# Graph channels and gate logits of a 16-group ViT tower kernel in fp16 passes, with a second ReLU for the high parts and a moved transpose step

## The chip, the cores and the metric

The kernel runs on one core of a Trainium2 chip. The metric is device time in microseconds, the median of several executions. PE is TensorE (PEld its weight loads), ACT ScalarE, DVE VectorE, POOL GpSimd, SP SyncE. TensorE's clock has two levels here, 2.4 and 1.2 GHz, which the profile shows as a granted clock of 1.00 and 0.50.

## The reference, cut to what matters

64 images of 2x104x104 become 169 tokens each of width 128, and a class token makes 170. Then two residual blocks follow:

```python
h = h + _L0_attn_ref(_layernorm(h, axis=-1), ...)
h = h + _L0_ffn_ref(_layernorm(h, axis=-1), ...)
```

The first is a graph convolution with 4 channels over the 128 features and a projection:

```python
h = jax.nn.relu(_gcn_conv(x, W1, b1, src, dst, norm))      # 4 channels
h = _gcn_conv(h, W2, b2, src, dst, norm)
x_combined = jnp.concatenate([x_enc[..., None], gcn_output], axis=-1)
x_projected = x_combined @ Wp.T + bp
```

The second is causal attention (2 heads of 64, normalised queries and keys) followed by a mixture of 8 experts of width 512, all of them computed and weighed by a softmax gate:

```python
gate = jax.nn.softmax(y @ gate_W + gate_b, axis=-1)
hid = jax.nn.gelu(jnp.einsum('bnd,edf->bnef', y, W1) + b1)
eo = jnp.einsum('bnef,efd->bned', hid, W2) + b2
out = jnp.einsum('bned,bne->bnd', eo, gate)
```

## The kernel before, in words

Features lie on the 128 partitions, tokens on the free axis. The 64 images are cut into 16 groups of 4 (T = 680 tokens, two halves of 340). A prologue of some 160 us builds all tokens (patch convolution) and folds the weights of the graph block into matrices: `adj` for the graph product, `plain` for the direct part and `gcn_m`, four 128x128 fp32 matrices, one for each channel. Then for each group g there is `attention(g)` and `ffn(g)`, written out for each engine as its own program; the order on an engine is the order of these calls, and semaphores tie them together. Groups 2 and on run in loops.

Most products are split by hand: an fp32 matrix becomes a high and a low fp16 part, and three fp16 passes (high by high, high by low, low by high) replace one fp32 product. Before the change the graph channels and the gate logits are still fp32.

The FFN is made of 32 slots, one for each 128-wide chunk of an expert's hidden layer, and 3 more (`LAG`). In slot s PE runs `experts_in(s)` (six products into one of two PSUM pairs, line 979), ACT runs a GELU into fp32 (line 620) and, in three slots of four, a second GELU into the fp16 high part (line 625, `hi`), DVE makes the low part (line 1395) and in the fourth also the high one, and PE runs `experts_out(s - 3)` (line 998). After each 4 chunks DVE weighs an expert's output (`weigh`, line 1408) and GpSimd adds it to the output by a DMA (line 459). In slots 32 and 33 PE runs the attention scores of the next group (`scores`, line 889), whose two PSUM pairs are free once the high GELUs of slots 30 and 31 are done.

Work for later groups hangs on the slots, by tables: `LN2_SLOTS` and `QK_SLOTS` (second layer norm, queries and keys of group g+1) and `EARLY_SLOTS` (fixing the tokens, first layer norm, graph product and ReLUs of group g+2). All of it shares one PSUM pair, `fr_ps`. An entry is run behind the slot's own work on each engine that has a part in it. `edges` (slot 28) leaves the graph product in `fr_ps`, and `relu0` to `relu3` read it on ACT (line 548), each with its own scale and bias, into `h1`.

`attention(g)` on PE is a list: `plain` and channel step 0 of group g+1 (line 759, all by way of `both`), `values` (line 871), step 1, the transposes of the probabilities of images 0 and 1 (`turn_probs`, line 904), step 2, `weigh(0)` (line 916), transposes, `weigh(1)`, transposes, step 3, `weigh(2)`, `project(0)` (line 923), `weigh(3)`, `mean2`, `project(1)` and then the logits (line 961), eight fp32 products of 85 tokens by 8 gates. On ACT it is 16 exponentials (line 584; they need DVE's maxima, and a table load goes ahead of the first), then a load of the GELU table, the evacuations of the attention output and of y, a square, and the tanh of the gates. On DVE it is `normalise(0)`, `normalise(1)`, the copies of the values, `normalise(2)`, the copies of the transposed probabilities, and so on; then `h2`, `y_parts` (y in fp16 parts, lines 1323 and 1325) and the softmax of the gates (lines 1354 to 1373). The transposes of image 0 wait for its normalised probabilities and for the first copy of the values. The first transposes of the layer norm roots (`cast_roots`, line 787) wait for DVE's inverse roots.

```python
                graph_of("plain", 0)
                for b in range(NB):
                    values(g, b, later)
                graph_of(1)
                turn_probs(g, 0)
                turn_probs(g, 1)
                graph_of(2)
                weigh(g, 0)
```

## Time and profile before

| what | value |
| --- | --- |
| median of 3 executions | 1547.23 us (1546.29 to 1547.50) |
| profiled execution, whole | 1546.54 us |
| its span | 1544.4 us |
| PE busy | 1480.5 us, 96% of the span |
| DVE busy | 1214.5 us, 79% |
| ACT busy | 1083.9 us, 70% |
| POOL busy | 192.8 us, 12% |
| chain of waits, share of PE | 67% |
| mean granted clock | 0.984 |

An engine's busy time is the union of its instructions. A row of the timeline gives the start of a run of instructions, its length, the engine and line, what is written from what, how many, and in brackets the idle time ahead of it with what ended it. PE rows overlap a little, since a matmul's end is modelled: the distance from one start to the next is the better price.

### The profile page before, as it was taken

The numbers are of one execution on the slowest core, as the hardware profiler recorded it, in microseconds if no ns is written. First come the engines' busy times: TensorE is split into PE (matmuls) and PEld (weight loads), VectorE is DVE, ScalarE is ACT, GpSimd is POOL, SyncE is SP. The second block draws the span as 40 slices with busy tenths as digits, with TensorE's granted clock in tenths as the row PEclk, the third lists the DMA queues.
The fourth block names the chain that finished last, engine by engine and source line by source line (L and its number), as shares of the span: only waits on it lengthen the run. The fifth ranks groups of instructions, "written<-read, shape, count | busy, mean of one in ns | idle before, by whom it ended". The sixth has DMA issues, their size and how long they took to land.

```text
span 1544.4 us, 31017 instructions
## 1 busy us (share of the span) xinstructions
PE 1480.5 (96%) x10879; PEld 1016.1 (66%) x10879; DVE 1214.5 (79%) x2567; ACT 1083.9 (70%) x1861; POOL 192.8 (12%) x223
## 2 busy tenths in 40 slices
PE   6898899999999999999999999999999999999998
PEld 4554666666666666666666666666666667667665
DVE  6768798878788787878788787888788787877765
ACT  5232577777777777786777777786777777777756
POOL 1134042010101010110101010110101010100101
PEclk9999899999999999999999999999999999999989
DMA  7866053333323242433233242433333242434334
GB/s 242 200 149 145 1 164 46 100 45 100 45 77 68 28 116 37 104 44 102 40 95 50 37 107 36 109 45 100 45 97 46 56 85 34 110 44 104 52 92 55
DMA packets 40339, 125.54 MB, mean 81 GB/s; under 512 B 5744, under 2 KB 5744, under 8 KB 38128
## 3 DMA queue, kind: packets, MB, share of 16 engines
q0 software_dynamic: 22464, 55.81, 26.0%
q1 hardware_dynamic: 17696, 69.28, 12.5%
q8 instruction: 19, 0.31, 0.1%
q14 instruction: 16, 0.13, 0.0%
q10 hardware_dynamic: 144, 0.01, 0.0%
HBM read 68.98 MB, written 50.48 MB: 77 GB/s over the span
## 4 chain that ended last, share of the span: by engine, by line
PE 67%; DVE 22%; issue 6%; ACT 4%; DVEq 1%; DMA 1%; POOLq 0%; ACTq 0%
PE pair L998 21%; PE pair L979 17%; PE pair L759 10%; DVE area L1395 6%; PE pair L746 4%; PE pair L916 3%; PE pair L904 2%; DVE root_t L1230 2%; PE pair L889 2%; DVE area L1408 2%; DVE area L1393 2%; PE pair L923 2%; PE pair L840 1%; PE pair L787 1%; PE pair L871 1%
## 5 line engine op out<-in xcount | busy, mean ns | idle before, releaser
L620 ACT ACTIVATE area<-pair,pack_b_sb 128x680 f32<-128x680 f32 x512 | 422.4, 828 | 219.6 <-PE pair L979 215.0
L1395 DVE TENSOR_TENSOR area<-area 128x680 f16<-128x680 f32 x512 | 445.5, 873 | 142.9 <-ACT area L625 138.2
L998 PE MATMUL pair<-area,ws 128*128 128x340 f16 x3072 | 527.2, 307 | 13.0 <-DVE area L1408 12.0
L979 PE MATMUL pair<-area,ws 128*128 128x340 f16 x3072 | 526.3, 308 | 0.4 <-ACT area L625 0.4
L998 PEld LDWEIGHTS pair<-area,ws 128*128 128x128 f16 x3072 | 286.8, 98 | 171.3 <-DVE area L1408 44.7
L979 PEld LDWEIGHTS pair<-area,ws 128*128 128x128 f16 x3072 | 297.3, 98 | 143.6 <-ACT area L625 0.5
L625 ACT ACTIVATE area<-pair,pack_b_sb 128x680 f16<-128x680 f32 x384 | 316.0, 823 | 0.0
L459 POOL DMA_DIRECT2D tower_out<-area x128 | 109.5, 855 | 1215.0 <-DVE area L1408 1162.9
L1408 DVE SCALAR_TENSOR_TENSOR area<-pair,pack_b_sb,area 128x340 f32<-128x340 f32 x256 | 134.0, 565 | 15.6 <-PE pair L998 15.3
L584 ACT ACTIVATE area<-pair,nbias,root 85x85 f32<-85x85 f32 (+1 forms) x256 | 112.3, 466 | 3.0 <-DVE nbias L1298 3.0
L746 PE MATMUL pair<-area,pack_a_sb 128*128 128x392 f32 (+1 forms) x260 | 96.0, 514 | 17.5 <-DVE area L1217 14.4
L746 PEld LDWEIGHTS pair<-area,pack_a_sb 128*128 128x128 f32 x260 | 50.9, 206 | 54.6 <-DVE area L1217 26.6
L759 PE MATMUL pair<-area,gcn_m 128*128 128x340 f32 x256 | 86.6, 462 | 0.0
L1393 DVE CAST area<-area 128x680 f16<-128x680 f32 x128 | 66.8, 522 | 20.6 <-ACT area L620 14.5
L548 ACT ACTIVATE area<-pair,pack_b_sb 128x680 f32<-128x680 f32 x64 | 59.1, 933 | 15.9 <-PE pair L759 15.3
L1217 DVE TENSOR_TENSOR area<-area,pack_a_sb 128x728 f32<-128x728 f32 x65 | 61.7, 996 | 0.3 <-PE pair L746 0.3
L598 ACT ACTIVATE area<-pair 128x340 f32<-128x340 f32 x32 | 14.5, 453 | 64.0 <-PE pair L923 64.0
L1310 DVE TENSOR_SCALAR area<-area,rs 85x85 f32<-85x85 f32 (+1 forms) x256 | 55.7, 278 | 2.3
L584 ACT ACTIVATION_READ_ACCUMULATOR area<-pair,nbias,root 85x1 f32 x256 | 55.2, 215 | 0.0
L528 ACT ACTIVATE ht<-pair 128x392 f32<-128x392 f32 (+1 forms) x26 | 19.8, 871 | 50.2 <-PE pair L746 50.2
L1317 DVE COPY area<-pair 85x510 f32<-85x510 f32 x64 | 42.4, 681 | 16.0 <-PE pair L904 16.0
L759 PEld LDWEIGHTS pair<-area,gcn_m 128*128 128x128 f32 x256 | 44.9, 192 | 13.9 <-issue 0.5
(209 smaller groups left out, 1634.4 us busy)
## 6 DMA issues: line engine op xcount, KB each, us to landing
tower_out<-area POOLq DMA_DIRECT2D x128, 340.0 KB, 4.6
area<-gate_scratch SPq DMA_DIRECT2D x16, 1360.0 KB, 10.0
area<-gate_scratch SPq DMA_DIRECT2D x16, 1020.0 KB, 7.2
area<-cells SPq DMA_DIRECT2D x16, 392.0 KB, 5.3
area<-cells POOLq DMA_DIRECT2D x14, 392.0 KB, 6.6
area<-area POOLq DMA_DIRECT2D x14, 392.0 KB, 4.8
tower_out<-ht SPq DMA_DIRECT2D x16, 340.0 KB, 2.3
area<-gate_scratch SPq DMA_DIRECT2D x16, 340.0 KB, 4.6
```

The costliest lines, as they stand in the source:

```text
L459: pool.dma_start(out[:, g * T:(g + 1) * T], tmp[e % 2], accum_op=ALU.add).then_inc(out_done, 16)
L584: nc.scalar.activation(probs[:, b * SCORE + o0:b * SCORE + o0 + w], score_ps_at(b)[:, h, c * QC:c * QC + w], ACT.Exp, bias=nbias[:, n:n + ...
L620: nc.scalar.activation(two(hid[slot % NHID]), halves(hid_ps[slot % 2]), ACT.Gelu_apprx_tanh, bias=col(COL_B1 + slot)).then_inc(hid_ready, 1)
L625: nc.scalar.activation(two(hh[slot % NPART]), halves(hid_ps[slot % 2]), ACT.Gelu_apprx_tanh, bias=col(COL_B1 + slot)).then_inc(hhi_act, 1)
L746: last = mm(cells_ps(p, j), conv_w[:, shift * D:(shift + 1) * D], xg[n % XG][:, c0 * BZ:c1 * BZ], start=(shift == 0), stop=(shift == SHIFT ...
L759: last = mm(fr_ps[:, j, 0:TH], lhs, rhs[:, j, :], start=start, stop=stop)
L979: last = mm(hid_ps[slot % 2][:, j, 0:TH], lhs[:, w], rhs[:, j * TH:(j + 1) * TH], start=(i == 0), stop=(i == 2))
L998: last = mm(eo_ps[:, j, 0:TH], lhs[:, w], rhs[:, j * TH:(j + 1) * TH], start=(m % CH == 0 and i == 0), stop=(m % CH == CH - 1 and i == 2))
L1217: v.tensor_tensor(xg[n % XG].rearrange("p (j b) -> p j b", b=BZ), src[:, c0 * BZ:(c0 + NP) * BZ].rearrange("p (j b) -> p j b", b=BZ), gv, ...
L1393: v.tensor_copy(hh[slot % NPART], hid[slot % NHID]).then_inc(hhi_dve, 1)
L1395: v.tensor_tensor(hl[slot % NPART], hid[slot % NHID], hh[slot % NPART], ALU.subtract).then_inc(hlo_ready, 1)
L1408: v.scalar_tensor_tensor(tmp[e % 2][:, j * TH:(j + 1) * TH], eo_ps[:, j, 0:TH], b2_s[:, e:e + 1], gbc[:, e * T + j * TH:e * T + (j + 1) * ...
```

## The change

- The four channel steps of groups 2 to 15 run in three fp16 passes: `gcn_h` and `gcn_l` by `h1_h` and `h1_l`. Groups 0 and 1 keep the fp32 path (`later` is false).
- For these groups ACT computes every ReLU twice, into fp32 buffers that are free then (`relu`) and into the fp16 high part `h1_h`. GpSimd subtracts the two into `h1_l` (`relu_parts`), channel 0 behind the output DMA of expert 5, channels 1 to 3 behind that of expert 6.
- The ReLUs move from slots 28, 29, 30, 31 to 29, 31, 32, 33; ACT's `ffn` now has 35 slots, the last three with no GELU.
- `fix0` and `fix1` move from slots 5 and 6 to 6 and 7.
- The logits leave `attention` for slot 0 of the FFN, by halves of four tiles, each ahead of that half's expert products: y_high by [W_high | W_low] (16 columns) and y_low by W_high (8 columns). They wait for `yl` and not for `y32`. DVE adds the two column groups with one more reduction.
- PE's `cast` of the second layer norm goes behind `experts_out` in its slot.
- `gcn_h`, `gcn_l` and `gate_hl` are made in the prologue, by GpSimd (two operations) and DVE (two).

```diff
--- before.py
+++ after.py
@@ -60,9 +60,9 @@
 GATE_SLOTS = {"turn": 2, "turned": 0}
 QK_SLOTS = {"q": 7, "sums_q": 9, "k": 9, "sums_k": 11, "root0": 11, "root1": 11, "root2": 12, "wide": 14,
             "cast": 16, "kn": 15}
-EARLY_SLOTS = {"fix0": 5, "fix1": 6, "fix2": 8, "fix3": 9, "tok_hi": 11, "mean": 18, "dev": 17, "sq": 19,
+EARLY_SLOTS = {"fix0": 6, "fix1": 7, "fix2": 8, "fix3": 9, "tok_hi": 11, "mean": 18, "dev": 17, "sq": 19,
                "var": 21, "root0": 21, "root1": 21, "root2": 22, "cast": 25, "xn": 24, "xn_lo": 25, "edges": 28,
-               "relu0": 28, "relu1": 29, "relu2": 30, "relu3": 31}
+               "relu0": 29, "relu1": 31, "relu2": 32, "relu3": 33}
 SUMS_AT = T // 2
 
 FIRST_0 = {"tail": 4, "fix0": 5, "fix1": 5, "fix2": 6, "fix3": 6, "mean": 7, "dev": 9, "sq": 10, "var": 11, "root0": 13,
...
@@ -209,8 +211,10 @@
 
         at[0] = 0
         dev, sq, h1 = take(T), take(T), take(4 * T)
+        h1_h, h1_l = (h1[:, 2 * n * T:2 * (n + 1) * T].bitcast(F16) for n in range(2))
         sqk, fix = h1[:, 0:T], h1[:, T:T + NB * NP * NP]
         xh, qs, kb, sqq = (take(T) for _ in range(4))
+        relu = (xh, sqq, dev, sq)
         xh_h, xh_l = take(T // 2).bitcast(F16), take(T // 2).bitcast(F16)
         part_h, part_l = take(T // 2).bitcast(F16), take(T // 2).bitcast(F16)
         k_wide = take(TILES * 128)[0:QC, :]
...
@@ -417,6 +422,11 @@
             def tokens_lo(g):
                 pool.wait_ge(tokh_ready, g - 1)
                 pool.tensor_tensor(two(part_l), tokens(g), two(part_h), ALU.subtract).then_inc(tokl_ready, 1)
+
+            def relu_parts(g, c):
+                half = slice(c * T, (c + 1) * T)
+                pool.wait_ge(h1_ready, 4 * g + c + 1)
+                pool.tensor_tensor(h1_l[:, half], relu[c], h1_h[:, half], ALU.subtract).then_inc(relu_lo, 1)
 
             def split(e):
                 pool.wait_ge(w_in[e], 32)
...
@@ -447,6 +457,10 @@
                     split(W_SPLIT.index(a))
             for e in range(len(W_SPLIT), 4):
                 split(e)
+            pool.wait_ge(dve_prep, PREP_DVE)
+            pool.tensor_copy(gcn_h[:, :], gcn_m[:, :]).then_inc(gcn_split, 1)
+            pool.wait_ge(gcn_split, 1)
+            pool.tensor_tensor(gcn_l[:, :], gcn_m[:, :], gcn_h[:, :], ALU.subtract).then_inc(gcn_split, 1)
 
             def weigh(g, later=True, ahead=True):
 
...
@@ -461,6 +475,9 @@
                         split(e + 4)
                     if e == 1 and ahead:
                         tokens_lo(g + 2)
+                    if e in (E - 3, E - 2) and ahead:
+                        for c in ((0,), (1, 2, 3))[e - E + 3]:
+                            relu_parts(g + 2, c)
 
             for g in range(G):
                 weigh(g, later=g > 0, ahead=g < G - 2)
...
@@ -533,7 +550,7 @@
                 nc.scalar.activation(root_in[:, ROOTS[kind]], fr_ps[0:QC, 0, first:first + n], ACT.Identity,
                                      bias=eps[0:QC, at:at + 1], scale=scale).then_inc(var_out[kind], 1)
 
-            def early(g, step):
+            def early(g, step, later=True):
                 if step == "tok_hi":
                     act.wait_ge(fixed, NB * (g + 1))
                     nc.scalar.activation(two(part_h), tokens(g), ACT.Copy).then_inc(tokh_ready, 1)
...
@@ -545,8 +562,11 @@
                 if step[:4] == "relu":
                     c = int(step[4])
                     act.wait_ge(g_ps, g + 1)
-                    nc.scalar.activation(two(h1[:, c * T:(c + 1) * T]), halves(fr_ps), ACT.Relu,
-                                         bias=scal[:, 4 + c:5 + c], scale=scal[:, c:c + 1]).then_inc(h1_ready, 1)
+                    dst = relu[c] if later else h1[:, c * T:(c + 1) * T]
+                    for part in (dst, h1_h[:, c * T:(c + 1) * T])[0:2 if later else 1]:
+                        last = nc.scalar.activation(two(part), halves(fr_ps), ACT.Relu,
+                                                    bias=scal[:, 4 + c:5 + c], scale=scal[:, c:c + 1])
+                    last.then_inc(h1_ready, 1)
 
             def graph(g, step):
                 if step == "sq2":
...
@@ -609,7 +629,7 @@
                 y_evac(g, 1)
                 if ahead:
                     graph(g + 1, "sq2")
-                act.wait_ge(lg_step, 3 * (g + 1))
+                act.wait_ge(lg_step, 4 * (g + 1))
                 nc.scalar.activation(lge[:, :], lg[:, :], ACT.Tanh, scale=0.5).then_inc(lge_ready, 1)
 
             def experts(g, slot):
...
@@ -626,8 +646,9 @@
                                          bias=col(COL_B1 + slot)).then_inc(hhi_act, 1)
 
             def ffn(g, ahead):
-                for slot in range(SLOTS):
-                    experts(g, slot)
+                for slot in range(SLOTS + LAG):
+                    if slot < SLOTS:
+                        experts(g, slot)
                     for step in steps_in(LN2_SLOTS, slot):
                         graph(g + 1, step)
                     for step in steps_in(QK_SLOTS, slot):
...
@@ -638,13 +659,13 @@
 
             def chain(n):
                 for step in steps_in(FIRST_0, n):
-                    early(0, step)
+                    early(0, step, later=False)
                 for step in steps_in(GRAPH_0, n):
                     graph(0, step)
                 for step in steps_in(QK_0, n):
                     queries_keys(0, step)
                 for step in steps_in(FIRST_1, n):
-                    early(1, step)
+                    early(1, step, later=False)
 
             sums_first()
             act.wait_ge(pack_b_in, 16)
...
@@ -808,16 +829,23 @@
                     pe.wait_ge(xnl_ready, g + 1)
                     of_xn(adj_h[:, :], adj_l[:, :]).then_inc(g_ps, 1)
 
-            def graph(g, step):
+            def graph(g, step, later=True):
                 if step == "plain":
                     pe.wait_ge(split_step, 4)
                     pe.wait_ge(h1_ready, 4 * (g + 1))
                     of_xn(plain_h[:, :], plain_l[:, :], stop=False)
-                if step in range(4):
+                if step in range(4) and later:
+                    w, src = slice(step * D, (step + 1) * D), slice(step * T, (step + 1) * T)
+                    pe.wait_ge(gcn_split, 2)
+                    pe.wait_ge(relu_lo, 4 * (g - 2) + step + 1)
+                    both(gcn_h[:, w], two(h1_h[:, src]), start=False, stop=False)
+                    both(gcn_h[:, w], two(h1_l[:, src]), start=False, stop=False)
+                    last = both(gcn_l[:, w], two(h1_h[:, src]), start=False, stop=(step == 3))
+                if step in range(4) and not later:
                     last = both(gcn_m[:, step * D:(step + 1) * D], two(h1[:, step * T:(step + 1) * T]),
                                 start=False, stop=(step == 3))
-                    if step == 3:
-                        last.then_inc(gcn_ps, 1)
+                if step == 3:
+                    last.then_inc(gcn_ps, 1)
                 if step == "mean2":
                     pe.wait_ge(h2_ready, g + 1)
                     both(mean_m[:, :], tokens(g)).then_inc(mean2_ps, 1)
...
@@ -931,7 +959,7 @@
                 def graph_of(*steps):
                     if ahead:
                         for step in steps:
-                            graph(g + 1, step)
+                            graph(g + 1, step, later)
 
                 if not later:
                     for m in range(NB // 2):
...
@@ -954,12 +982,15 @@
                 graph_of("mean2")
                 project(g, 1)
 
-                pe.wait_ge(pt_ready, NB * (g + 1))
-                for t in range(TILES):
-                    if t % NB == 0:
-                        pe.wait_ge(y_ready, 2 * g + t // NB + 1)
-                    last = mm(eo_ps[0:QC, 0, t * E:(t + 1) * E], y32[:, t * QC:(t + 1) * QC], gate_ws,
-                              start=True, stop=True)
+            def logits(g, j):
+
+                if j == 0:
+                    pe.wait_ge(pt_ready, NB * (g + 1))
+                pe.wait_ge(yl_ready, 2 * g + j + 1)
+                for t in range(j * NB, (j + 1) * NB):
+                    c, y = 2 * t * E, slice(t * QC, (t + 1) * QC)
+                    mm(eo_ps[0:QC, 0, c:c + 2 * E], yh[:, y], gate_hl[:, :], start=True, stop=False)
+                    last = mm(eo_ps[0:QC, 0, c:c + E], yl[:, y], gate_hl[:, 0:E], start=False, stop=True)
                 last.then_inc(logit_ps, 1)
 
             def experts_in(g, slot):
...
@@ -974,7 +1005,7 @@
                 w = slice(slot * D, (slot + 1) * D)
                 for j in range(2):
                     if slot == 0:
-                        pe.wait_ge(yl_ready, 2 * g + j + 1)
+                        logits(g, j)
                     for i, (lhs, rhs) in enumerate(((w1h, yh), (w1h, yl), (w1l, yh))):
                         last = mm(hid_ps[slot % 2][:, j, 0:TH], lhs[:, w], rhs[:, j * TH:(j + 1) * TH],
                                   start=(i == 0), stop=(i == 2))
...
@@ -1006,7 +1037,8 @@
                     if slot < SLOTS:
                         experts_in(g, slot)
                         for step in steps_in(LN2_SLOTS, slot):
-                            graph(g + 1, step)
+                            if step != "cast":
+                                graph(g + 1, step)
                         for step in steps_in(GATE_SLOTS, slot):
                             gates(g, step)
                         for step in steps_in(QK_SLOTS, slot):
...
@@ -1018,12 +1050,14 @@
                         scores(g + 1, slot - SLOTS, True)
                     if slot >= LAG:
                         experts_out(g, slot - LAG)
+                    if slot == LN2_SLOTS["cast"]:
+                        graph(g + 1, "cast")
 
             def chain(n):
                 for step in steps_in(FIRST_0, n):
                     early(0, step, later=False)
                 for step in steps_in(GRAPH_0, n):
-                    graph(0, step)
+                    graph(0, step, later=False)
                 for step in steps_in(QK_0, n):
                     queries_keys(0, step)
                 for step in steps_in(FIRST_1, n):
...
@@ -1103,6 +1137,10 @@
                     v.tensor_copy(hi[:, :], src).then_inc(split_step, 1)
                     dve.wait_ge(split_step, 2 * p - 11)
                     v.tensor_tensor(lo[:, :], src, hi[:, :], ALU.subtract).then_inc(split_step, 1)
+                if p == 9:
+                    v.tensor_copy(gate_hl[:, 0:E], gate_ws).then_inc(split_step, 1)
+                    dve.wait_ge(split_step, 9)
+                    v.tensor_tensor(gate_hl[:, E:2 * E], gate_ws, gate_hl[:, 0:E], ALU.subtract).then_inc(split_step, 1)
                 if p == 7:
                     v.tensor_scalar(gq[:, 0:1], col(COL_QN), float(DH) ** 0.5, None, ALU.mult).then_inc(dve_prep, 1)
                     dve.wait_ge(dve_prep, 21)
...
@@ -1349,13 +1387,15 @@
                     graph(g + 1, "dev2")
                 y_parts(g, 1)
 
-                dve.wait_ge(logit_ps, g + 1)
+                dve.wait_ge(logit_ps, 2 * (g + 1))
                 lg3 = lg[:, :].rearrange("p (t e) -> p t e", e=E)
-                v.tensor_tensor(lg3, eo_ps[0:QC, 0, 0:TILES * E].rearrange("p (t e) -> p t e", e=E),
-                                gate_bs.unsqueeze(1).broadcast_to([QC, TILES, E]), ALU.add).then_inc(lg_step, 1)
-                dve.wait_ge(lg_step, 3 * g + 1)
+                v.tensor_reduce(lg3, eo_ps[0:QC, 0, 0:2 * TILES * E].rearrange("p (t n e) -> p t e n", n=2, e=E),
+                                AX.X, ALU.add).then_inc(lg_step, 1)
+                dve.wait_ge(lg_step, 4 * g + 1)
+                v.tensor_tensor(lg3, lg3, gate_bs.unsqueeze(1).broadcast_to([QC, TILES, E]), ALU.add).then_inc(lg_step, 1)
+                dve.wait_ge(lg_step, 4 * g + 2)
                 v.tensor_reduce(gm[:, 0:TILES], lg3, AX.X, ALU.max).then_inc(lg_step, 1)
-                dve.wait_ge(lg_step, 3 * g + 2)
+                dve.wait_ge(lg_step, 4 * g + 3)
                 v.tensor_tensor(lg3, lg3, gm[:, 0:TILES].unsqueeze(2).broadcast_to([QC, TILES, E]),
                                 ALU.subtract).then_inc(lg_step, 1)
                 dve.wait_ge(lge_ready, g + 1)
```

## Rows read from the trace of the kernel before

**Rows 1.** A steady group's stretch: us, busy of PE, PEld, DVE, ACT, POOL, clock, DMA.

```profile
773.00:859.00 86.00, 84.71 (x660) 58.80 (x658) 69.36 (x150) 64.91 (x112) 8.30 (x9) 1.00 0.35 69
```

**Rows 2.** Timeline of the first attention, ACT and PE: start us, us, engine, line.

```profile
168.41 0.42 ACT L584 ACTIVATE area<-pair,nbias,root 85x85 f32<-85x85 f32 x1
...
173.88 1.99 PE L904 MATMUL pair<-ident,area 85*85 85x85 f32 x12 [4.48 <-DVE area L1329]
175.66 2.54 PE L759 MATMUL pair<-area,gcn_m 128*128 128x340 f32 x4
...
185.72 1.48 PE L961 MATMUL pair<-pack_b_sb,area 128*85 128x8 f32 x16
```

**Rows 3.** Timeline of the last attention, ACT and PE.

```profile
1459.30 0.42 ACT L584 ACTIVATE area<-pair,nbias,root 85x85 f32<-85x85 f32 x1
...
1464.76 1.60 PE L904 MATMUL pair<-ident,area 85*85 85x85 f32 x12 [2.43 <-DVE area L1329]
...
1476.66 2.37 PE L961 MATMUL pair<-pack_b_sb,area 128*85 128x8 f32 x16
```

**Rows 4.** Timeline of ACT at the end of a steady FFN.

```profile
768.72 0.92 ACT L548 ACTIVATE area<-pair,pack_b_sb 128x680 f32<-128x680 f32 x1
769.52 0.83 ACT L620 ACTIVATE area<-pair,pack_b_sb 128x680 f32<-128x680 f32 x1
770.23 0.84 ACT L625 ACTIVATE area<-pair,pack_b_sb 128x680 f16<-128x680 f32 x1
...
773.16 0.97 ACT L548 ACTIVATE area<-pair,pack_b_sb 128x680 f32<-128x680 f32 x1
774.14 1.28 ACT L584 ACT_TABLE_LOAD   x1
775.64 0.42 ACT L584 ACTIVATE area<-pair,nbias,root 85x85 f32<-85x85 f32 x1 [0.21 <-DVE nbias L1298]
```

**Rows 5.** Timeline of PE over the attention that follows it.

```profile
771.51 1.12 PE L889 MATMUL pair<-area 64*85 64x85 f32 x16
...
776.95 0.74 PE L759 MATMUL pair<-area,plain_h 128*128 128x340 f16 x4
777.82 1.30 PE L759 MATMUL pair<-area,gcn_m 128*128 128x340 f32 x4
778.97 0.28 PE L871 MATMUL pair<-wv_h,area 128*85 128x128 f16 x2
...
781.50 1.07 PE L904 MATMUL pair<-ident,area 85*85 85x85 f32 x12
...
786.00 1.34 PE L759 MATMUL pair<-area,gcn_m 128*128 128x340 f32 x4
787.28 0.66 PE L916 MATMUL pair<-area 85*64 85x170 f32 x8
...
791.04 1.48 PE L961 MATMUL pair<-pack_b_sb,area 128*85 128x8 f32 x16
...
794.11 1.30 PE L771 MATMUL pair<-mean_m,area 128*85 128x1 f32 x16
```

**Rows 6.** Same timeline, DVE; then two groups by line: busy, mean ns, idle before.

```profile
792.10 0.51 DVE L1325 TENSOR_TENSOR area<-area 128x340 f16<-128x340 f32 x1
...
L787 PE MATMUL pair<-ident,root 85*128 85x85 f32 x256 | 24.8, 240 | 8.0 <-DVE root L1234 8.0
...
L419 POOL TENSOR_TENSOR area<-ht,area 128x680 f16<-128x680 f32 x14 | 20.6, 1470 | 18.7 <-ACT area L539 18.7
```

**Rows 7.** PE idle in the prologue, and stretches of 1 us with the clock.

```profile
66.69 6.96 PE L746 MATMUL pair<-area,pack_a_sb 128*128 128x392 f32 x12 [1.73 <-ACT ht L528]
...
66.00:67.00 1.00, 0.31 (x1) 0.34 (x2) 1.00 (x3) 1.00 (x3) 0.00 (x0) 0.52 0.90 276
...
178.00:179.00 1.00, 1.00 (x10) 0.71 (x9) 0.00 (x0) 0.00 (x0) 0.00 (x0) 0.67 0.00 0
...
1482.00:1483.00 1.00, 1.00 (x7) 0.59 (x6) 0.97 (x2) 0.52 (x1) 0.00 (x0) 0.72 0.00 0
```

More of the change, by code:

```diff
@@ L140, in vit_tower @@
         gate_ws, gate_bs, b2_s = packs["gate_w"], packs["gate_b"][0:QC, :], packs["b2"]
+        gate_hl = sb("gate_hl", [128, 2 * E], F16)
         area = sb("area", [128, AREA])
@@ L157, in vit_tower @@
         gcn_m = sb("gcn_m", [128, 4 * D])
+        gcn_h, gcn_l = (sb(n, [128, 4 * D], F16) for n in ("gcn_h", "gcn_l"))
         gcn_c = sb("gcn_c", [128, 1])
@@ L264, in vit_tower @@
         g_ps, h1_ready, gcn_ps, h2_ready = map(sem, ("g_ps", "h1_ready", "gcn_ps", "h2_ready"))
+        relu_lo, gcn_split = map(sem, ("relu_lo", "gcn_split"))
         mean2_ps, dev2_ready, sq2_ready, var2_ps = map(sem, ("mean2_ps", "dev2_ready", "sq2_ready", "var2_ps"))
```

## The prediction

> **What bounds the kernel now.** I read the table of stretches first: in one steady group PE is busy 84.71 of 86.00 us at a granted clock of 1.00 (2.4 GHz), DVE 69.36, ACT 64.91 [rows 1]. The exponentials of the first and of the last group start 1290.9 us apart [rows 2, 3], 86.06 us for each of 15 groups, and nearly all of that is PE. Then I read the end of one FFN and the attention after it in the timeline, on ACT [rows 4] and on PE [rows 5]. The reader should see that the exponentials are already on the edge. In the steady group they start at 775.64 and PE begins the transposes of the first probabilities at 781.50, 5.86 us later [rows 4, 5]. In the first and last attention, where PE stands waiting for them (idle 4.48 and 2.43 us), the distance is 5.47 and 5.46 us [rows 2, 3]: four exponentials, four more, two normalisations, one copy of the values, all in order. So the steady group has 0.4 us of slack there, and a later exponential soon becomes PE's wait.
>
> **Graph channels.** A channel step was two fp32 products of two records each, four records: 777.82 to 778.97, 1.15 us [rows 5]. Three fp16 passes are six records like the three passes ahead of it (776.95 to 777.82, 0.87 us). Saved are 0.29 us a step, and 0.41 us where the fp32 step held up the weights behind it (step 3: 786.00 to 787.28 is 1.28 us). The new path is taken in 14 attentions (g = 1 to 14): at least 14 x 4 x 0.29 = 16 us, if PE stays the bound.
>
> **The ReLUs on ACT.** Four become eight. One takes 0.80 us from start to start (768.72 to 769.52 [rows 4]). The f16 copy may be nearer a GELU's 0.71 us; I take 0.80, since the nearest row is the same ReLU. Before, relu1 and relu2 sit between hi(29) and GELU(31), and relu3 follows hi(31). After, relu0's two lie before GELU(30), and GELU(31) starts where it did. But hi(30), which scores(0) waits for, moves from 770.23 to 771.03 and ends at 771.87, while scores(0) started at 771.51 [rows 5]: PE waits 0.4 us. After hi(31) there were one ReLU, the table load and the first exponential. Now there are six: first at 773.16, last at 777.16, table load at 778.14, exponential at 779.42. The exponentials start **3.8 us later**; before, nothing but the maxima (0.21 us of idle) held them [rows 4].
>
> **What PE does meanwhile.** It reaches `plain` at 777.4 (776.95 and the 0.4), waits for the last ReLU until 778.2, and runs plain 0.87, step 0 0.87, values 1.33 (the 2.53 us between 778.97 and 781.50 [rows 5], less a step of 1.20, between the two seen), step 1 0.87: done at 782.15. It can transpose at 779.42 + 5.47 = 784.9, so it idles 2.7 us, and that stage starts **3.4 us late**. Steps 0 and 1 save time only inside this wait. Step 2 is swallowed too, since `weigh` behind it waits for the probabilities. Step 3 gives back 0.4. The logits' place comes 3.0 us late.
>
> **GpSimd.** Four subtractions like the one at 1.47 us [rows 6]. relu_parts(0) has its input near 770.3, before attention begins; parts 1 to 3 end near 779.6 (778.14 + 1.47), and the step that needs part 1 comes at 781.3, the others after the wait. Queued behind them on GpSimd is only expert 7's output DMA, up to 1.5 us late; what it frees is written again for expert 1 of the next FFN, slots later. Without that cover a group would pay up to the 1.5. The two preparations of gcn_h and gcn_l and DVE's two small ones lie in a prologue where GpSimd idles: nothing. The bound on the other side is the next row: 4 x 1.47 on the path, 5.9 us a group, for which I see no way.
>
> **Logits.** Before: 16 fp32 records from 791.04, then slots 0 and 1 of the FFN, until 794.11: 3.07 us [rows 5], of which 12 products take 12 x 0.145 = 1.73 and the records 1.34. After: eight fp16 records for a half, 0.45 us (0.056 each: `values` has 24 such weights in 1.33; the fp32 record's 0.084 is the upper bound), three products 0.43, then the second half, which waits for yl. That comes with DVE's subtraction, 792.10 + 0.51 = 792.61 [rows 6], 1.6 us after the start. So 1.62 + 0.45 + 0.43 + 0.87 = 3.37 us: 0.3 **lost**, not gained. The DVE chain to the gates could start at 792.61 and now starts 0.7 us later (791.04 + 2.07 + the matmul's end, 0.2), with one small reduction more, a shape no row has: I put it at 0.25, half of that 0.51 us subtraction, from nothing to the whole, so gates, GELU(0) and out(0) come about 1.0 us later. Queued behind the new wait for yl are only the second half of slot 0 and what follows it.
>
> **Cast.** The eight transposes waited 8.0 us in 15 groups [rows 6], 0.53 each. Behind experts_out(1) that wait is gone, and covers about what the later gates cost: at slot 5 PE is 0.25 behind before. The extra products ahead of the transposes delay hx by less than DVE's own lag. fix0 and fix1 change places on DVE, which has 16.6 us free a group [rows 1]: nothing, and if DVE were late at weigh(0), at most the lag of 1.0 us.
>
> **Sum without the clock:** 3.41 - 0.41 + 0.25 = 3.25 us a group, x 14 = 45.5.
>
> **The clock.** An idle stretch of 1.73 us in the prologue left the clock at half (mean 0.52 in that microsecond), so did the 4.48 and the 2.43 [rows 2, 3, 7]. I expect 2.7 us, with 0.8 just before, to do it in most groups. In the first attention the clock came back during 178 to 179 (0.67), 4.5 us after PE resumed. There PE took 11.84 us from transposes to logits, against 9.54 in the steady group [rows 2, 5]: 2.30 more. A step at half clock was 2.47 there and will be 1.73 in fp16, so 1.56 us a group, x 14 = 21.8.
>
> **Total:** 45.5 + 21.8 = 67.3. The profiled execution took 1546.54 (span 1544.4 and 2.1 around it): 1613.8. The median of three is 0.7 above it, so I say **1615 us**. From both sides: if f16 ReLUs take 0.71, 14 x 3 x 0.09 = 4 us less; if no group loses the clock, 22 less.
>
> **A rule weighed.** The table load takes 1.28 us, 774.14 to 775.42, and the first exponential starts at 775.64 as soon as the maxima are there; at the end it starts at 1459.30, 0.02 after the load. The Trainium skill, "ScalarE: Activation LUTs", section "What ACT_TABLE_LOAD costs", adds a drain of about 1380 ns to each switch. By it the exponentials would start 1.38 us later still, 19 us in all, 1634. The rows show no such time after the load; I go by the rows.
>
> **Rivals.**
> - *The clock stays low.* In the last attention PE also resumed after 2.43 us, and the clock came back only in 1482 to 1483 (0.72), 17 us later [rows 7]; transposes to logits took 11.90 us with no graph work in it. For it: fp16 steps give PE shorter stretches of dense work than the fp32 step that stood before the return in the first attention. Against it: the last one has idle gaps that graph work fills. From transposes to logits 9.54 - 0.8 = 8.7 us of work would double; if the clock returns with the dense products just before the logits, some 6.9 of it: 14 x (3.25 + 6.9) = 142 us, 1689. Chance 0.22, and part of it would show as a time between 1615 and 1689.
> - *No fall.* 1592 us. For it: 2.7 us lies between busy stretches at full clock. Chance 0.18.
> - *Faster: the exponentials do not decide.* Place: PE's wait for the first transposes. It decides as soon as ACT's extra work is above the 0.4 us of slack. If it stayed below (ReLUs overlapped with PE's other work, the table load off the path), PE would keep its 16 us and the 8 of the cast: 1523. Against it: in-order ACT with six ReLUs ahead. Chance 0.07, with 0.01 of it within 0.2%.
> - *Change without effect*: it would need the ReLUs to stand behind the exponentials; the ACT program has slots 32 and 33 ahead of attention. Under 0.01.
>
> The forecast itself has 0.53.
>
> **Range.** From 1586, below the case without a fall by 3 us for cheaper ReLUs and 3 for logits, to 1685, just inside the worst of the low clock. About 3 us, 0.2%, is what a measurement can tell from no change. Faster 0.06, within 0.01, slower 0.93.
>
> **What would show it.** Right: exponentials starting 3.8 us after where they stood relative to hi(31), six ReLU rows before the table load; a PE wait near 2.7 us at L904's counterpart, in 14 groups; windows of half clock in the attentions; logits in two parts with a wait for yl; no wait at the ln2 transposes; group period near 91 us. Wrong: a steady PE busy share of 98% as before, or fp16 steps standing unbroken in front of transposes that wait for nothing.

## The result, and the profile after

The changed kernel takes **1622.85 us** (median of 4, 1615.83 to 1630.71) against 1547.03 for the one before. The ratio, estimated from the single executions, is 1.0497, 95% interval 1.0473 to 1.0521. The forecast was 1615 in a range of 1586 to 1685.

The profile page of the changed kernel, its span and parts 1 and 2 (the clock in tenths):

```profile
span 1621.4 us, 31400 instructions
PE 1498.3 (92%) x10991; PEld 1011.4 (62%) x10991; DVE 1233.3 (76%) x2585; ACT 1125.5 (69%) x1917; POOL 276.3 (17%) x281
...
PEclk9998999999989999999999899999999899999989
```

PE's busy time is 18 us longer (1498.3 for 1480.5), though it has less to do: in a version below with the same products, whose clock held, it is 1461.4. Its share of the longer span has fallen from 96% to 92%. So the 77 us by which the span grew (1621.4 for 1544.4) are time in which PE waits or runs at half clock.

The end of an FFN and the attention after it in the changed kernel, ACT and PE, the counterpart of [rows 4] and [rows 5]. The last line is PE at the second half of the logits:

```profile
342.56 1.12 PE L917 MATMUL pair<-area 64*85 64x85 f32 x16 [0.35 <-ACT area L645]
343.07 0.87 ACT L645 ACTIVATE area<-pair,pack_b_sb 128x680 f16<-128x680 f32 x1
343.79 5.01 ACT L567 ACTIVATE area<-pair,pack_b_sb 128x680 f32<-128x680 f32 x6
...
348.81 1.28 ACT L604 ACT_TABLE_LOAD   x1
348.85 0.75 PE L780 MATMUL pair<-area,plain_h 128*128 128x340 f16 x4 [0.68 <-ACT area L567]
349.44 0.45 PE L780 MATMUL pair<-area,plain_l 128*128 128x340 f16 x2
349.73 0.74 PE L780 MATMUL pair<-area,gcn_h 128*128 128x340 f16 x4
350.11 0.42 ACT L604 ACTIVATE area<-pair,nbias,root 85x85 f32<-85x85 f32 x1
...
355.57 1.19 PE L932 MATMUL pair<-ident,area 85*85 85x85 f32 x12 [2.60 <-DVE area L1367]
...
366.33 0.21 PE L992 MATMUL pair<-gate_hl,area 128*85 128x16 f16 x1 [0.71 <-DVE area L1363]
```

The last high GELU of the FFN in the kernel before:

```profile
772.45 0.86 ACT L625 ACTIVATE area<-pair,pack_b_sb 128x680 f16<-128x680 f32 x1
```

In the changed kernel six ReLUs stand in a row behind the last high GELU (343.07), then the table load, then the first exponential (350.11), 7.04 us after that GELU's start. Before, it was 3.19 us (772.45 to 775.64 [rows 4]). PE waits four times: 0.35 us at the first scores, 0.68 at `plain`, 2.60 at the first transposes, which start 5.46 us after the exponentials, and 0.71 at the second half of the logits.

All 14 changed attentions show these rows. They differ in what follows. From the transposes to the first logits took 9.14 us in five of them, 12.1 in six and 15.3 in three; before it was 9.54. Stretches of two attentions; the clock is in the third column from the right:

```profile
534.00:545.00 11.00, 8.37 (x89) 6.51 (x88) 7.51 (x27) 9.73 (x36) 1.66 (x2) 1.00 0.22 32
...
446.00:452.00 6.00, 6.00 (x37) 4.24 (x36) 3.59 (x10) 2.42 (x5) 0.00 (x0) 0.53 0.00 0
452.00:458.00 6.00, 6.00 (x25) 3.33 (x24) 1.89 (x4) 1.00 (x2) 0.00 (x0) 0.50 0.00 0
```

The first line is an attention without a fall (its transposes start at 540.07). The other two are one whose transposes start at 444.76, whose clock fell at 446.4 and came back only 13.7 us later. The distance from one attention's exponentials to the next is 89.12 us where the clock held, some 92.1 and 95.3 where it fell, 86.03 before.

The span's 77.0 us, by those distances: 13 x 3.09 = 40.2 without the clock; 36.4 from it (6 x 2.98 + 3 x 6.18); 7.2 in the interval of the first FFN; 0.2 and 1.0 less in the last two stretches; and 5.5 **less** in the prologue, up to the first exponential.

Of the 7.2 us in the first FFN, 3.8 are the ReLUs, 2.1 a longer wait for DVE's weigh of one expert (4.74 for 2.62), and behind that wait the clock was at 0.50 from 218 to 221, which it was not before. That leaves 1.3 us for it; a fall of this length cost 1.5 in a kernel below:

```profile
218.06 1.88 PE L1029 MATMUL pair<-area,ws 128*128 128x340 f16 x6 [4.74 <-DVE area L1448]
...
218.00:221.00 3.00, 2.94 (x11) 1.61 (x12) 2.96 (x3) 1.25 (x2) 2.14 (x3) 0.50 0.35 32
```

### The profile page after: what moved, and what is told of

Same layout as the page of the kernel before. It is cut to its first block, busy times and chain, and to the rows that moved or that the text cites. A ratio compares the mean times of both kernels' runs of the same rounds, so it can differ in the third digit from the quotient of the medians.

```text
span 1621.4 us, 31400 instructions
## 1 busy us (share of the span) xinstructions
PE 1498.3 (92%) x10991; PEld 1011.4 (62%) x10991; DVE 1233.3 (76%) x2585; ACT 1125.5 (69%) x1917; POOL 276.3 (17%) x281
## 4 chain that ended last, share of the span: by engine, by line
PE 59%; ACT 16%; DVE 16%; issue 7%; DMA 1%; DVEq 0%; ACTq 0%; POOLq 0%
PE pair L1010 18%; PE pair L1029 18%; PE pair L780 7%; ACT area L567 5%; ACT area L645 4%; ACT area L604 3%; PE pair L767 3%; DVE area L1435 3%; PE pair L944 3%; PE pair L932 3%; ACT area L640 2%; PE pair L808 2%; PE pair L951 2%; DVE root_t L1268 2%; DVE area L1448 2%
## 5 line engine op out<-in xcount | busy, mean ns | idle before, releaser
L640 ACT ACTIVATE area<-pair,pack_b_sb 128x680 f32<-128x680 f32 x512 | 422.4, 828 | 222.1 <-PE pair L1010 220.3
L1029 PE MATMUL pair<-area,ws 128*128 128x340 f16 x3072 | 528.0, 308 | 16.0 <-DVE area L1448 12.1
L567 ACT ACTIVATE area<-pair,pack_b_sb 128x680 f32<-128x680 f32 x120 | 101.0, 962 | 15.3 <-PE pair L780 15.3
L767 PE MATMUL pair<-area,pack_a_sb 128*128 128x392 f32 (+1 forms) x260 | 91.2, 493 | 17.8 <-DVE area L1255 14.7
L429 POOL TENSOR_TENSOR area<-area 128x680 f16<-128x680 f32 x56 | 82.3, 1470 | 122.4 <-ACT area L567 118.5
L932 PE MATMUL pair<-ident,area 85*85 85x85 f32 x384 | 51.2, 288 | 43.3 <-DVE area L1367 43.3
L932 PEld LDWEIGHTS pair<-ident,area 85*85 85x85 f32 x384 | 42.7, 190 | 53.5 <-DVE area L1348 48.5
L944 PEld LDWEIGHTS pair<-area 85*64 85x64 f32 x512 | 39.1, 172 | 29.7 <-issue 16.9
```

The source lines that it names most:

```text
L567: last = nc.scalar.activation(two(part), halves(fr_ps), ACT.Relu, bias=scal[:, 4 + c:5 + c], scale=scal[:, c:c + 1])
L640: nc.scalar.activation(two(hid[slot % NHID]), halves(hid_ps[slot % 2]), ACT.Gelu_apprx_tanh, bias=col(COL_B1 + slot)).then_inc(hid_ready, 1)
L767: last = mm(cells_ps(p, j), conv_w[:, shift * D:(shift + 1) * D], xg[n % XG][:, c0 * BZ:c1 * BZ], start=(shift == 0), stop=(shift == SHIFT ...
L932: last = tr(eo_ps[0:QC, b % 2, n * QC:(n + 1) * QC], probs[:, b * SCORE + n * QC:b * SCORE + (n + 1) * QC], ident[0:QC, 0:QC])
L1029: last = mm(eo_ps[:, j, 0:TH], lhs[:, w], rhs[:, j * TH:(j + 1) * TH], start=(m % CH == 0 and i == 0), stop=(m % CH == CH - 1 and i == 2))
```

## The experiments

Distances between exponentials ("group") are worked out from each kernel's timeline as above. They are less disturbed than the medians: the first exponential starts anywhere from 162.9 to 169.4 us in the twelve profiled kernels, and the wait in the first FFN lasts from 2.6 to 4.7 us, with no visible relation to the change that was made. Each kernel has one profiled execution, so waits, groups and falls of the clock are those of that one.

### A busy PE in place of the wait

```diff
                 graph_of(1)
+                if ahead and later:
+                    for _ in range(9):
+                        both(zero_h[:, :], two(h1_h[:, T:2 * T]), start=False, stop=False)
                 turn_probs(g, 0)
```

> The changed kernel, with 18 fp16 products of a zero matrix (2.6 us) put behind channel step 1 in 14 groups, into the sum that is open there, so that PE is busy where it waited 2.60 us and nothing else moves. If the low clock is what the five groups of 89.1 us lack and the nine of 92.1 and 95.3 have, all groups take 89.1 us and the time is 1623 - 36 = 1587 us, with low clock only in the first and last attention. If the low clock costs nothing because ACT and DVE set the pace there, the time stays at 1620 or above.

Measured: 1587.58 us (1585.8 to 1590.24), ratio 1.0272 (1.0242 to 1.0302). The added products and what follows, one attention:

```profile
441.45 2.77 PE L782 MATMUL pair<-area,zero_h 128*128 128x340 f16 x18
444.22 1.19 PE L934 MATMUL pair<-ident,area 85*85 85x85 f32 x12
...
438.00:456.00 18.00, 17.25 (x158) 12.25 (x157) 11.96 (x35) 11.99 (x40) 1.80 (x2) 1.00 0.14 19
```

The transposes still start 5.47 us after the exponentials, so nothing ahead of them moved. The clock stays at 1.00 in all 14, every transposes-to-logits distance is 9.14 and a group takes 89.1. So the low clock costs 35 us, it comes from PE's standing idle there, and the late exponentials themselves stay.

### Two ReLUs fewer on ACT

```diff
-                    for part in (dst, h1_h[:, c * T:(c + 1) * T])[0:2 if later else 1]:
+                    for part in (dst, h1_h[:, c * T:(c + 1) * T])[0:2 if later and c < 2 else 1]:
...
+                if c >= 2:
+                    pool.tensor_copy(h1_h[:, half], relu[c]).then_inc(relu_hi, 1)
+                    pool.wait_ge(relu_hi, 2 * (g - 2) + c - 1)
```

> The changed kernel, with the high parts of channels 2 and 3 made by a cast on GpSimd and not by a second ReLU on ACT: two ReLUs fewer between the last GELU and the exponentials. If the exponentials' start sets the attention, they come 1.6 us sooner, PE's idle before the transposes falls from 2.60 to 1.0 us, the clock stays at 1.00 and a group takes 89.1 - 1.6 = 87.5 us: 1547 + 14 x 1.5 and some 3 us in the first FFN, 1571 us. If the subtractions on GpSimd or the fp16 steps were the cost, the time stays above 1610.

Measured: 1582.27 us, the median of 1578.49, 1581.92, 1582.62 and one execution of 1856.62, which the ratio of 1.022 (1.0184 to 1.0256) leaves out. A group without a fall took 87.56 us: 1.56 less for two ReLUs, as the exponentials' start says. But the clock fell in 8 of 14:

```profile
354.66 1.19 PE L935 MATMUL pair<-ident,area 85*85 85x85 f32 x12 [1.69 <-DVE area L1370]
...
354.00:360.00 6.00, 5.34 (x40) 3.86 (x40) 4.68 (x15) 3.73 (x13) 0.00 (x0) 0.72 0.32 50
```

I had taken the 1.6 us off the idle time at the transposes alone. The 0.68 at `plain` went first, and 1.69 us stayed in one piece, after which the clock could still fall. Six falls cost 1.5 us each and two 3.0: 15 us together, which covers the miss of 11.

### The eight ReLUs back in slots 28 to 31

```diff
-               "relu0": 29, "relu1": 31, "relu2": 32, "relu3": 33}
+               "relu0": 28, "relu1": 29, "relu2": 30, "relu3": 31}
```

> The changed kernel, its eight ReLUs put back to slots 28 to 31. The second ReLUs of slots 29 and 30 now push the last GELU back by 1.6 us, but only two ReLUs stand behind it. If the exponentials' start is what counts, and not where the ReLUs stand, they come 1.6 us sooner than in the changed kernel, as with two ReLUs fewer: 87.5 us for a group without low clock. PE's idle is split (0.4 and 0.7 us at the scores, some 1.0 at the transposes), so the clock should fall in few groups: 1571 us, below the 1582 of the kernel with two ReLUs fewer. If the last GELU's lateness costs as much as the exponentials', 1590 us or more.

Measured: 1571.32 us (1567.74 to 1573.85), 1.0163 (1.0136 to 1.019). One attention:

```profile
694.90 1.12 PE L917 MATMUL pair<-area 64*85 64x85 f32 x16 [0.36 <-ACT area L645]
697.96 1.12 PE L917 MATMUL pair<-area 64*85 64x85 f32 x16 [0.65 <-ACT area L645]
706.59 1.19 PE L932 MATMUL pair<-ident,area 85*85 85x85 f32 x12 [1.02 <-DVE area L1367]
```

The same number of ReLUs as in the changed kernel, in the old slots, costs 51 us less than in the new ones. A group took 87.81, 1.31 less than the 89.12 of the changed kernel, and the clock fell in none of the 14. So the *place* of the ReLUs is the larger part of the loss only with the clock: it is worth 1.31 of the 3.09 us a group, and all of the 36 us of low clock.

The split of a wait seems to matter beside its sum. Here PE waits 2.23 us in four pieces (0.36, 0.65, 1.02, and 0.20 at `values`), with no fall in 14; with two ReLUs fewer it waited 2.04 us in two (0.35 and 1.69), with 8 falls in 14.

### No second ReLU: both parts on GpSimd

```diff
-                pool.tensor_tensor(h1_l[:, half], relu[c], h1_h[:, half], ALU.subtract).then_inc(relu_lo, 1)
+                pool.tensor_copy(h1_h[:, half], relu[c]).then_inc(relu_hi, 1)
+                pool.wait_ge(relu_hi, 4 * (g - 2) + c + 1)
+                pool.tensor_tensor(h1_l[:, half], relu[c], h1_h[:, half], ALU.subtract).then_inc(relu_lo, 1)
...
-                        for c in ((0,), (1, 2, 3))[e - E + 3]:
+                        for c in ((0, 1), (2, 3))[e - E + 3]:
```

ACT runs the four fp32 ReLUs alone, in slots 28 to 31.

> The changed kernel without any second ReLU: ReLUs back in slots 28 to 31, high and low parts both on GpSimd (a cast of about 1.2 us and the 1.47 us subtraction, four times, two behind expert 5's output and two behind expert 6's). The exponentials then start where they did before. PE cannot transpose sooner than 5.47 us after them (5.87 before), and the rest to the logits takes 9.14 for 9.54: 0.8 us a group gained, 0.1 lost with the logits: 85.3 us a group, 1547 - 10 = 1537 us, no low clock but in the first and last attention. Rival: GpSimd is too slow for the steps of the channels, PE waits for the fourth part and the time is 1550 or more.

Measured: 1542.37 us, 0.9983 (0.9969 to 0.9996), 85.80 us a group (85.3 expected; below, where the 0.5 went). Then the same with the old logits, in fp32 and in their old place:

> As the kernel with both parts on GpSimd, with the logits in fp32 in their old place. With the moved transposes the new logits cost only 0.1 us a group by the changed kernel's trace, so this is 1535 us. If they cost the 0.97 us a group that they cost alone, it is 1522 us.

Measured: **1530.94 us** (1526.87 to 1533.31), 0.9899 (0.9872 to 0.9925), 84.82 us a group. So the fp16 logits cost 0.98 us a group here, the second of the two expected cases. The median fell by 11 us and not by 15 or more; of the two profiled executions, this kernel's was 4.4 us longer in the prologue and the first FFN. This version is faster than both kernels. One attention of it:

```profile
683.22 0.96 ACT L567 ACTIVATE area<-pair,pack_b_sb 128x680 f32<-128x680 f32 x1
683.72 1.98 POOL L430 TENSOR_TENSOR area<-area 128x680 f16<-128x680 f32 x1
684.20 1.28 ACT L603 ACT_TABLE_LOAD   x1
685.65 0.74 POOL L428 CAST area<-area 128x680 f16<-128x680 f32 x1
686.47 1.47 POOL L430 TENSOR_TENSOR area<-area 128x680 f16<-128x680 f32 x1
687.01 0.95 DVE L1328 SCALAR_TENSOR_TENSOR nbias<-mx,root 85x8 f32<-85x8 f32 x1
687.88 1.04 DVE L1438 SCALAR_TENSOR_TENSOR area<-pair,pack_b_sb,area 128x340 f32<-128x340 f32 x2
688.85 0.16 DVE L1333 RECIPROCAL rs<-sm 85x4 f32<-85x4 f32 x1
...
691.65 1.19 PE L931 MATMUL pair<-ident,area 85*85 85x85 f32 x12 [0.52 <-DVE area L1359]
```

The same place in the kernel before:

```profile
776.86 0.16 DVE L1298 SCALAR_TENSOR_TENSOR nbias<-mx,root 85x8 f32<-85x8 f32 x1
776.96 1.05 DVE L1408 SCALAR_TENSOR_TENSOR area<-pair,pack_b_sb,area 128x340 f32<-128x340 f32 x2
777.93 0.16 DVE L1303 RECIPROCAL rs<-sm 85x4 f32<-85x4 f32 x1
```

GpSimd is in time for every step, and PE waits for none of its parts. But PE now waits 0.5 us at the transposes, which start 5.87 us after the exponentials and not the 5.47 expected. The last channel's subtraction on GpSimd lies beside DVE's work here. DVE's small product of the maxima (`nbias`) takes 0.95 us for 0.16 and ends at 687.96, 0.02 after the subtraction (686.47 + 1.47). The weigh of the last expert, the normalisations and the copy of the values, which the transposes wait for, stand behind it in DVE's order: the copy starts 5.03 us after the exponentials, against 4.64 before.

An attention has two such products. One of them is held in two other kernels as well, each time to the end of a subtraction on GpSimd within 0.02 us: the second for 1.02 us with two ReLUs fewer, the first for 0.75 with the ReLUs in the old slots, where the exponentials wait for it 0.3 us behind the table load (the 87.81 us a group for the 87.5 expected). The weigh is not the cause of the late copy: in that last kernel it stands in the same place, 1.4 us behind the exponentials' start, but the second product takes 0.16, and the transposes start at 5.47. So the fp16 steps ahead of the transposes gain nothing here because GpSimd's work makes DVE 0.4 us later; the 0.40 us behind them (9.14 for 9.54) is all they give. A kernel that keeps the subtraction away from that product was not tried; by these rows it would have 0.4 us a group to win, an estimate.

### The logits and the moved transposes, alone and together

The logits alone in the kernel before (the hunks of the diff that name `gate_hl`, `logits`, `lg_step`):

> The kernel before, with the logits alone in fp16 by halves. My term: the wait for the low part of y costs PE 0.3 us a group and the gates come 1.0 us later, so the wait at the roots' transposes (0.53 now) grows: 0.3 to 1.3 us in 16 groups, 1552 to 1567 us. Rival, the fp16 records themselves decide: 16 records at 0.04 us for 16 at 0.084 give 0.7 us a group, 1536 us.

Measured: 1563.05 us (1559.14 to 1563.39), 1.0104 (1.0082 to 1.0126), 87.00 us a group, 0.97 more.

DVE carries it. The last operation on the gates (the counterpart of line 1373) starts 20.47 us after the exponentials, against 19.51 before, and from there to weigh(0), the weigh of the first expert, it is 11.33 us in both kernels, of which DVE is idle for 0.8. So weigh(0) comes 0.96 us later too, and PE waits for it.

The moved transposes alone (the two hunks with `"cast"` in PE's `ffn`):

> The kernel before, with the one step moved: PE's transposes of the second layer norm's roots go behind experts_out in slot 4. My term for it was 0.53 us of PE wait in 15 groups. If that wait was PE's own, it is gone and nothing takes its place: 1547 - 8 = 1539 us. Rival: DVE is not earlier by it, so weigh(0) in slot 6 comes no sooner and PE loses at experts_out(4) what it gained: within 2 us of 1547, with the idle time in front of line 998's products (13.0 us now) up by about 8.

Measured: 1545.78 us, 0.9988 (0.9971 to 1.0004), 86.03 us a group: the rival that was named with it. Groups by line, first one of the kernel before, then two of this one:

```profile
L998 PE MATMUL pair<-area,ws 128*128 128x340 f16 x3072 | 527.2, 307 | 13.0 <-DVE area L1408 12.0
```

```profile
L998 PE MATMUL pair<-area,ws 128*128 128x340 f16 x3072 | 527.2, 307 | 23.4 <-DVE area L1411 22.4
...
L787 PE MATMUL pair<-ident,root 85*128 85x85 f32 x256 | 24.0, 236 | 0.0
```

The 8.0 us in front of line 787 [rows 6] are gone, and in front of line 998 there are 23.4, 10.4 more than the 13.0 before, put down to DVE's weigh: in a steady group PE's wait at weigh(0) has grown from 0.35 to 1.11 us, and weigh(0) starts 30.85 us after the exponentials in both kernels. Both changes together:

> The kernel before, with the logits by halves and the moved transposes, nothing else. Alone the logits cost 16.8 us and the moved transposes gave nothing. If the moved transposes cover the later gates (experts_out(1) runs while PE would wait), the two together cost 0.1 to 0.25 us a group: 1548 to 1551 us. If they only add, 1563 us.

Measured: 1558.18 us (1555.38 to 1564.09), 1.0088 (1.0065 to 1.0112), and again 87.00 us a group. The moved transposes cover nothing of the logits' cost either.

### fix0 and fix1 one slot later

```diff
-EARLY_SLOTS = {"fix0": 5, "fix1": 6, ...
+EARLY_SLOTS = {"fix0": 6, "fix1": 7, ...
```

> The kernel before, with fix0 and fix1 one slot later and nothing else. I had priced this at nothing. If DVE is what weigh(0) waits for, its two operations of 0.4 us ahead of it are gone and so is PE's 0.35 us wait at experts_out(4): 85.7 us a group for 86.03, 1541 us, the idle time in front of line 998's products down from 13.0 to about 8. If my price was right: 86.0 and 1546.

Measured: 1537.09 us (1533.31 to 1541.68), 0.9927 (0.991 to 0.9944), 85.45 us a group. With the moved transposes:

> The kernel before, with the moved transposes and the moved fix0 and fix1. The moved transposes alone gave 0, since what PE gained came back as its wait for weigh(0). With DVE's fix0 out of the way the gain should stay: 0.53 + 0.35 less something, 85.2 us a group and 1534 us. If the two were independent, it is the time of fix0 moved alone.

Measured: 1533.92 us (1532.65 to 1536.55), 0.9916 (0.9901 to 0.9931), 85.13 us a group. The groups by line of the kernel with fix0 and fix1 alone, and of the one with both:

```profile
L998 PE MATMUL pair<-area,ws 128*128 128x340 f16 x3072 | 526.4, 307 | 9.2 <-DVE area L1408 8.2
```

```profile
L998 PE MATMUL pair<-area,ws 128*128 128x340 f16 x3072 | 527.6, 308 | 12.7 <-DVE area L1411 11.6
```

The two operations of fix0 stood right in front of weigh(0) on DVE:

```profile
805.58 0.39 DVE L1241 SCALAR_TENSOR_TENSOR area<-conv_u,img,conv_b 128x169 f32<-128x169 f32 x1
806.17 0.40 DVE L1244 SCALAR_TENSOR_TENSOR ht<-ht,img,area 128x169 f32 x1 [0.20 <-DVE area L1241]
806.49 1.04 DVE L1408 SCALAR_TENSOR_TENSOR area<-pair,pack_b_sb,area 128x340 f32<-128x340 f32 x2
```

Without them weigh(0) starts 0.9 us sooner, of which PE gains 0.58. With fix0 out of DVE's way the moved transposes keep 0.32 us of their 0.53. Together these two small changes are worth 0.90 us a group, 0.8%. They are in the version with both parts on GpSimd and the old logits as well: of the 1.21 us a group that it gains on the kernel before, 0.90 are theirs, and 0.31 (84.82 against 85.13) are the fp16 channel steps. The two versions were each set against other runs of the kernel before; the intervals of their ratios overlap, and by the medians alone which is the faster stays open.

## Why the prediction was right, point by point

- **The exponentials, 3.8 us late.** Right. From the last high GELU's start to them it was 7.04 us for 3.19, and in a group without a fall the whole stretch from logits to exponentials grew by 3.89 us (89.12 - 5.47 - 9.14 against 86.03 - 5.87 - 9.54). Two ReLUs fewer gave 1.56 us back, and the table load's end is the exponential's start (348.81 + 1.28 = 350.09, 350.11), without the 0.21 us for the maxima that stood there before. The Trainium skill, "ScalarE: Activation LUTs", section "What ACT_TABLE_LOAD costs", adds a drain to the load; this trace has 0.02 us there and does not agree.
- **PE's waits.** 0.4, 0.8 and 2.7 us forecast, 0.35, 0.68 and 2.60 found. The distance of 5.47 us was the right price.
- **The slack of 0.4 us** was there: in the kernel before, DVE's copy of the values starts 4.64 us after the exponentials, as in the kernels where PE waits and transposes at 5.47. With the exponentials in their old place PE still waits until 5.87, since GpSimd's subtraction makes DVE 0.4 us later.
- **GpSimd hidden.** Right for the changed kernel: PE waits for none of its parts, and the product that it lengthens there (0.38 us for 0.16) stands ahead of the exponentials, where DVE has time. It is not so where GpSimd makes both parts: the 0.4 us above are its price.
- **Step 3 gives back 0.4, steps 0 to 2 nothing.** Right: 9.14 for 9.54 behind the transposes, with PE idle ahead of them.
- **Logits 0.3 lost, transposes covering it, fix0 and fix1 nothing.** The sum, 0.25 us a group, was near the 0.09 that the changed kernel's trace leaves, and that was luck: all three terms were wrong, and by the single runs they cancel (0.97 lost, 0.90 gained). The wait for y's low part at the second half was 0.71 us, against 0.74 as worked out (1.62 - 0.88), and the gates did come 1.0 us late. But that lateness does not stay inside DVE: it reaches weigh(0) whole. The transposes gained nothing while fix0 stood ahead of weigh(0). And fix0 and fix1, priced at nothing because DVE has free time in the group, were worth 0.58. The failed step is the argument from DVE's free 16.6 us [rows 1]: hardly any of it lies between the gates and weigh(0) (0.8 us in 11.3), and weigh(0) is what PE waits for next. The prediction named a late DVE at weigh(0) as a bound and left it out of the sum.
- **Sum without the clock:** 3.25 forecast, 3.09 found.
- **The clock.** Forecast as 1.56 us in each of 14 groups, 22 us in all; found as 0 in five, 2.98 in six and 6.18 in three, 36 us. The rival "no fall" was right for five groups and "the clock stays low" in part for three, so the forecast case is an average over cases, none of which cost 1.56.
- **The miss.** The clock's term was 14.6 us too small and the others together 1.7 (in the main the first FFN's 7.2 for 3.25). Against that stood 5.5 us less in the prologue and 1.0 at the end, in no term of the forecast, and the prologue differs by as much between kernels that share it (162.90 us here, 168.20 with the ReLUs in the old slots). Without these the profiled execution would have missed by 16 us and not by 10 (the median missed by 8): that much of the near hit is luck.
- **The rival of a faster kernel** needed ACT's extra work to stay off the path. The nearest to it is the version with both parts on GpSimd, at 1542, and with the old logits 1531, not 1523.

## What to carry to other kernels

Before giving a second pass to an engine with 25% free time, look at what stands behind it in that engine's own order: here two ReLUs of 0.80 us between the last GELU and the exponentials were 1.56 us of the group. The ReLUs among the GELUs cost less, and GpSimd's copies cost less still, though not nothing: DVE was held by one of them. So before moving work to an idle engine, look also at which operations of its neighbour it will lie beside. And price small moves by the next wait of the stretch, not by the free share of a group.

## What was not expected

- An idle stretch of one length does not always end the same way. After 2.60 us the clock held in 5 of 14 attentions and fell in 9; after 1.69 us it held in 6 and fell in 8; no fall followed the 1.02 us. The prologue's wait of 1.73 us, followed by half clock before the change [rows 7], left it alone in the changed kernel. What sets one apart from the other is not shown. These falls are the likely reason for the changed kernel's spread of 15 us in 4 executions, against 8 in 17 of the kernel before (1541.55 to 1549.29) and 4.4 in 4 of the filler kernel. Its fastest execution had a mean granted clock of 0.966, its slowest 0.958. By an estimate from these two, that is 27 us more at half clock; with 2.98 us lost for each 6.8, it makes some 12 of the 15 us.
- In three attentions the clock stayed low for 13.7 us with PE busy all the time, where it came back after 6.8 in the others.
- A cast of 128x680 to f16 on GpSimd took 0.74 to 1.04 us, less than the 1.2 I expected, and the fp16 logits came every 0.04 us, not 0.056. Neither shows in the time: PE waits for no part of GpSimd's, and the second half of the logits waits for y's low part.
- The first FFN of the changed kernel waited 4.74 us for the weigh of one expert, the kernel before 2.62. The change does not set this: the filler kernel, the same up to there but for a matrix of zeros made in the prologue, waited 2.75. Why it differs from one execution to the next is open.
